# Half of the mode weights, and the loads queued behind them, issued only once the first mix operand exists

## The reference

```python
x = x + L0(_gn(x))     # _gn: every channel of every image to mean 0, variance 1
x = x + L1(_gn(x))

# L0: spectral convolution
x_ft = rfftn(x, axes=(-2, -1))
blk  = einsum('bimn,hiomn->bhomn', x_ft[:, :, :32, :32], weight)   # a 32 x 32 channel matrix per mode (m, n)
xr   = irfftn(blk put into zeros, s=(64, 64))
out  = einsum('bchw,oc->bohw', xr, fc_w) + fc_b

# L1: 3x3 convolution with a kernel of its own for each image
att  = softmax(sigmoid(mean(x) @ ksm_w.T))                  # 16 candidates
cw   = einsum('bk,koihwc->boihwc', att, dft_weight)         # given as a 3x3 spectrum
out  = (conv(x, clip(ifft2(cw).real), padding 1) + bias) * fbm_scale
```

## Time and profile before

| | before |
|---|---|
| time, median of 3 runs | 139.57 us (138.45 to 140.53) |
| span of the profiled execution | 137.8 us |
| time outside the span, against the median | 1.8 us |
| instructions in the span | 4822 |
| PE busy | 122.5 us, 89% of the span; 2060 matmuls and 2060 weight loads |
| VectorE busy | 87.8 us, 64% |
| ScalarE busy | 70.7 us, 51% |
| GpSimd busy | 52.8 us, 38% |
| moved by DMA | 25.17 MB, mean 183 GB/s |

### The profile page before, as it was taken

How to read it: one execution, slowest core, us unless ns; L and a number is a source line. 1 busy time by engine, 2 the same in 40 slices (tenths; PEclk the granted TensorE clock), 3 DMA queues, 4 the chain that set the end, 5 groups by cost and what they waited for, 6 DMA issues and landing times.

```text
span 137.8 us, 4822 instructions
## 1 busy us (share of the span) xinstructions
PE 122.5 (89%) x2060; PEld 91.8 (67%) x2060; DVE 87.8 (64%) x201; ACT 70.7 (51%) x143; POOL 52.8 (38%) x44
## 2 busy tenths in 40 slices
PE   0799997969997969979999979989999999999970
PEld 0799997869996959979999969873323432223230
DVE  0077696879996743553357685999873789922340
ACT  0468458538965336523317775644998329311100
POOL 7993000009999999999600550130500000000000
PEclk9999999999999999999999999999999999999997
DMA  3999999999500036787876899887989968884477
GB/s 90 268 272 257 233 222 357 302 384 399 204 5 7 0 81 156 171 203 165 181 164 153 172 178 153 180 202 164 168 184 175 211 156 189 195 191 105 104 162 143
DMA packets 71892, 25.17 MB, mean 183 GB/s; under 512 B 67904, under 2 KB 68160, under 8 KB 71872
## 3 DMA queue, kind: packets, MB, share of 16 engines
q1 hardware_dynamic: 70784, 24.62, 77.2%
q10 hardware_dynamic: 1088, 0.26, 0.9%
HBM read 14.38 MB, written 4.19 MB: 135 GB/s over the span
## 4 chain that ended last, share of the span: by engine, by line
PE 86%; issue 5%; DVE 3%; DMA 2%; ACT 0%; SPq 0%
PE slot L1050 27%; PE slot L882 14%; PE slot L963 11%; PE slot L978 8%; PE slot L941 6%; PE slot L952 5%; PE slot L908 3%; PE aggp L1008 3%; PE slot L904 3%; DMA x_buf<-x 2%; PE small L904 1%; PE aggp L904 1%; DVE kern L780 1%; PE aggp L941 1%; PE small L892 1%
## 5 line engine op out<-in xcount | busy, mean ns | idle before, releaser
L1050 PE MATMUL slot<-y_buf,conv_w 128*32 128x512 f32 (+1 forms) x136 | 31.7, 603 | 0.0
L1050 PE MATMUL slot<-w_buf,conv_w 128*32 128x512 f32 (+1 forms) x136 | 31.7, 603 | 0.0
L882 PE MATMUL slot<-cst,x_buf 128*64 128x64 f32 x512 | 19.0, 241 | 5.3 <-DMA x_buf<-x 4.5
L882 PEld LDWEIGHTS slot<-cst,x_buf 128*64 128x64 f32 x512 | 18.4, 154 | 5.6 <-issue 5.5
L821 DVE TENSOR_TENSOR bd_buf<-slot,q_buf 128x512 f32<-128x512 f32 (+1 forms) x17 | 11.0, 670 | 9.3 <-PE slot L1050 9.1
L1050 PEld LDWEIGHTS slot<-y_buf,conv_w 128*32 128x32 f32 x136 | 8.3, 109 | 12.6 <-issue 12.0
L441 POOL TENSOR_TENSOR x_buf<-y_buf 128x1024 f32<-128x1024 f32 x4 | 7.7, 1934 | 22.5 <-DVE y_buf L709 22.5
L978 PE MATMUL slot<-cst,t_buf 128*128 128x128 f32 x128 | 15.5, 278 | 0.8 <-issue 0.8
L978 PEld LDWEIGHTS slot<-cst,t_buf 128*128 128x128 f32 x128 | 14.7, 192 | 1.4 <-issue 1.2
L963 PE MATMUL slot<-cst,r_buf 128*64 128x128 f32 x256 | 14.6, 274 | 0.7 <-ACT r_buf L491 0.7
L613 DVE TENSOR_REDUCE row_sq<-q_buf 128x16 f32<-128x1024 f32 (+1 forms) x9 | 9.8, 1097 | 7.7 <-ACT q_buf L459 7.7
(11 more groups left out here) (128 smaller groups left out, 222.7 us busy)
## 6 DMA issues: line engine op xcount, KB each, us to landing
x_buf<-x SPq DMA_DIRECT2D x16, 256.0 KB, 4.3
w_buf<-w_modes SPq DMA_DIRECT2D x16, 256.0 KB, 5.0
x_buf<-x SPq DMA_DIRECT2D x32, 128.0 KB, 3.1
w_buf<-y_buf SPq DMA_DIRECT2D x16, 256.0 KB, 5.9
out<-bd_buf SPq DMA_DIRECT2D x28, 128.0 KB, 2.8
t_buf<-dft_w SPq DMA_DIRECT2D x4, 288.0 KB, 5.3
t_buf<-x_buf SPq DMA_DIRECT2D x8, 128.0 KB, 2.4
r_buf<-x_buf SPq DMA_DIRECT2D x8, 128.0 KB, 3.4
```

The costliest lines, as they stand in the source:

```text
L882: last = pe.matmul(ps[64 * ri:64 * ri + 64, col:col + 64], x_part(k)[:, i, q, :], const("fwd_h")[:, 64 * ri:64 * ri + 64], start=True, sto ...
L1050: last = pe.matmul(ps[32 * j:32 * j + 32, 32 * u0:32 * u1], cw[r][:, b, k, :], src, start=(k == terms[0][0]), stop=(k == terms[-1][0]))
```

## The change

SyncE's program gets one wait. Before the loads of the third ml (mix 2) it waits until VectorE has counted the first operand. The first eight loads of mode weights and the late constants stay where they were; the last eight, the four of `dft_w` and the one of `params` stand behind the new wait, since SyncE issues in order.

```diff
             for ml in range(4):
+                if ml == 2:
+                    sp.wait_ge(bd_ready, 1)
                 for q in range(4):
                     sp.dma_start(modes[:, ml, 8 * q:8 * q + 8].rearrange("p n xo -> p (n xo)"), w_modes[ml, q]
                                  ).then_inc(modes_in[ml], 16)
```

## The result

The changed kernel takes 141.18 us (median of 6 runs, 140.85 to 143.03), the kernel before 139.01 us in the same count (138.01 to 140.61). The ratio is 1.0161, 95% interval 1.0117 to 1.0204, so slower by some 2.2 us, 1.6 to 2.8; whether by more than 2% is left open. The profiled execution has a span of 139.1 us and a time of 140.91, 1.8 us outside the span as forecast.

The account below looks back on a forecast made before the run. PE was taken to bound the kernel, with 86% of the span. The span of 137.8 plus 1.9 for late instruction blocks gave 139.7, and 1.8 us outside it made 141.5 us, range 138.5 to 143.0.

Parts of the forecast that it names:

- The bound, and the holes as missing instructions: PE holds 86% of the span; its "issue" holes of 0.72, 1.22 and 0.85 us are waits for instruction blocks.
- The wait, the landing times, the readers: SyncE resumes at about 31.2 us, last moved byte lands at 42.2, four readers of moved data cost nothing.
- The cover: GpSimd's twelfth step ends at 58.2 us, copies waiting for it start at 61.28: 3 us left.
- The hole before 30.17: PE's early hole of 1.22 us stays, taken as 0; a gain of 1.22 at most kept for the range.
- The later blocks: PE's instruction blocks near 40 and 43 us come late behind moved loads: +1.1 to +3.4 us, taken +1.9.
- case B: Early hole goes, later ones grow: PE resumes at 44.3 to 45.4, +1.1 to +2.2, taken +1.3, 140.9 us; chance 0.20.
- case A: Hole before 30.17 stays, blocks near 40 and 43 late: +1.1 to +3.4, taken +1.9, 141.5 us; chance 0.42.
- The clock: PE's granted clock, 1.00 in each stretch, was not lowered by holes of up to 1.2 us; no cost forecast.
- Theory 2: In the experiments: a late reader, above all GpSimd with its candidate kernels, holds VectorE or copies; +1 us or more.
- the theory: In the experiments: transfers delay PE's instruction blocks; the change removes one delay and makes two.

Follow-up runs that it names:

- GpSimd late: Kernel before with GpSimd's chain on the candidate kernels held until the fifth mix count, transfers unchanged: 139.67, 137.20 and 139.89 us beside 139.28 for before.
- the eight loads left out: Changed kernel without its last eight mode loads, mix 2 and 3 reading the weights of mix 0 and 1: 138.41 us, ratio 0.9929 to before.
- candidate kernels ahead: Changed kernel with the candidate kernel loads and params issued ahead of the new wait, only eight mode loads behind it: 140.12 us, ratio 1.0064 to before.
- before with moved block ends: Kernel before with 16 small products (32 matmuls) added ahead of PE's first work: 139.84 us, ratio 1.0063.
- wait at the last f1: Changed kernel with SyncE waiting for the last f1 instead of the first mix operand: 140.37 us, ratio 1.0066 to before.
- staggered: Changed kernel, but mix 2's loads, candidate kernels and params wait for the last f1, mix 3's for half of mix 1: 139.90 us, ratio 1.0032 to before.
- staggered with moved block ends: The staggered kernel plus 16 small products at PE's start, run twice: 138.80 us, ratio 0.9965, and 140.78 us, ratio 1.0036, to before.
- half of the change: Changed kernel with the wait ahead of only the last four mode loads, mix 2's going out as before: 140.79 us, ratio 0.9959 to before.
- the second measurement: The changed kernel itself, unaltered, measured once more against the kernel before: 141.99 us, ratio 1.0126.
- the changed kernel with moved block ends: Changed kernel plus 16 small products at PE's start: 140.94 us, ratio 1.0081 to before.
- the three with moved block ends among the first eight kernels: 16 small products added at PE's start to the kernel before, the wait at the last f1 and the changed kernel: ratios 1.0063, 1.0083, 1.0081 to before.
- the last: Second run of staggered with moved block ends, against the kernel before: 140.78 us, ratio 1.0036.

## Why the prediction was right, and where it was wrong

*The bound, and the holes as missing instructions.* Right. Moving the program by 32 matmuls moved the holes by 31 or 32, in two kernels.

*The wait, the landing times, the readers.* The wait ended at 31.46 (31.2 forecast), the lull and the busy stretch were there, no engine but GpSimd waited for a moved load. `params`, issued at 37.11 with 6.6 us to landing, was there at 43.7 and read at 46.55; the candidate kernels landed at 43.5, 1.3 us later than the sum had it, and GpSimd's twelfth step ended at 59.3 against 58.2, with the copies at 62.7. The cover held, as the kernel with GpSimd late shows.

*The hole before 30.17.* This is the step that failed: "I take 0, since what was issued first should move first". It went, in both profiles of the changed kernel and with the eight loads left out. In those three, where nothing but the late constants was issued between the request and 30 us, the packet started 2.3 to 3.0 us after it. In four kernels more loads were issued over 1 us ahead of the packet (before, GpSimd late, candidate kernels ahead, before with moved block ends), and it took 3.2 to 4.2 us. That points to traffic issued after the request, but it doesn't prove it. In four others the next loads were issued less than 1 us ahead of the packet or behind it, and can hardly have moved (loads issued at 30.21 moved nothing until 31.0): wait at the last f1 3.5 us, staggered 3.7, staggered with moved block ends 3.2, half of the change 2.2. So 2.2 to 3.7 us without later traffic stand against 3.2 to 4.2 with it, and why the early packet came sooner stays open. What is shown is its price: PE's block lasts 5.4 us (23.55 to 28.95), the packet and the time behind it take 2.4, so a packet that starts within 3.0 us costs nothing.

The Trainium skill (DMA: Bandwidth & Descriptors, Queues, rings and completion order) has each DMA engine take turns between queues, a packet of about 9 to 17 descriptors at a time. If a row of 2 KB is one descriptor, at 82 ns (399 GB/s over 16 engines), a turn is an estimated 0.7 to 1.4 us by that page's figure, not nothing as the prediction had it. On top of the idle 1.1 us that would cover the delays up to about 2.5 us and not those of 2.8 to 4.2. Whether the rest lies in the DMA engines or in memory no run here shows.

*The later blocks.* Right in place, and by the mechanism named. The packets that the prediction had counted back to 36.8 and 40.4 are in the trace of the kernel before, in the windows of 0.1 us from 36.8 and from 40.4:

```profile
q8 instruction: 1, 0.02, 54.9%
q8 instruction: 1, 0.02, 84.4%
```

They start at 36.84 and 40.41, and PE reaches the blocks before at 36.3 and 40.2, so a block is asked for some tenths ahead of PE's own work where PE is not starved. In the changed kernel the packet at 38.2 falls within the 37.7 to 38.7 of case B, PE resumed at 40.65 (40.0 to 41.5) and at 44.81 (44.3 to 45.4). What happened is thus case B, given 0.20 and taken at +1.3 and 140.9 us: +1.2 us in the profile beyond the late start. The forecast was case A's, and that its 141.5 lies as near to the median of 141.18 as B's 140.9 is luck. Its +1.9 stood for the two late blocks alone, whose holes grew by 1.36 + 1.06 = 2.4 us, and it left out the 1.22 us that the early hole gave back. Nor is all of the hole in mix 2 the traffic's: with GpSimd late, with the eight loads left out and with the wait at the last f1, where the engines moved 5 to 7 GB/s by then, it was 1.45, 1.29 and 1.47 us. A block that PE enters starved is asked for only then, and that alone costs a hole in the mix.

*The clock.* "Holes of up to 1.2 us did not lower it" was true of the rows and no ground for longer ones. Of the first runs of the changed kernel three had granted clocks of 0.996 to 1.000 and spans of 139.1 to 139.4 us, and those with 0.976 and 0.964 had 140.6 and 141.2; but one with 0.984 had 139.1. In the profile with 0.982, that of the second measurement, half clock cost 1.1 us of PE's own time. Up to 56 us it fell in six profiles, each time behind a hole of 1.31 to 2.59 us in the mix or the `f2` beside it; holes of 1.30 to 2.01 us in other places or profiles were not followed by it. The Trainium skill (TensorE: Matmul & The Clock Gate, What's actually happening) says that the throttled state is the default and activity lifts it, with 1.2 and 2.4 GHz as the only two levels; the 0.50 to 0.52 of these stretches agree. This may account for the upper ones of the changed kernel's runs; how much of its median it makes is not settled.

*Theory 2.* Small, and its mechanism is in the rows. `bconst` at 1.16 us instead of 0.16 delayed `fc` by 0.2 us in the profile after, and 0.17 with GpSimd late alone. VectorE's step and the step of GpSimd beside it, before and after:

```profile
49.01 0.16 DVE L687 TENSOR_TENSOR bconst<-prm 128x1 f32<-128x1 f32 x1
48.18 1.25 POOL L399 TENSOR_SCALAR bd_buf<-bd_buf 128x384 f32<-128x384 f32 x1
...
50.58 1.16 DVE L689 TENSOR_TENSOR bconst<-prm 128x1 f32<-128x1 f32 x1
50.50 1.22 POOL L398 TENSOR_TENSOR bd_buf<-t_buf,bd_buf 128x384 f32<-128x384 f32 x1
```

The slow step ends with GpSimd's. So it is in all 14 profiles: in five GpSimd ran a TENSOR_TENSOR there (after, the changed kernel again and with moved block ends, GpSimd late, half of the change), and `bconst` took 0.74 to 1.16 us, up to its end; in nine it was at its TENSOR_SCALAR steps, and `bconst` took 0.16. `fc_diag` ended 0.1 to 0.3 us behind GpSimd's TENSOR_TENSOR in all 14. The late candidate kernels cost these tenths by moving GpSimd's TENSOR_TENSOR steps beside `bconst`.

*What stays open.* Single holes scatter by 0.5 us and more with the same transfers, so that holes of one profile predict a ratio only to about 0.5%. No kernel here removes the traffic from both critical places and keeps all loads in time, and of those that the theory had faster than before, only the one without its last eight loads was. What makes a packet late beyond full engines, and how much of the 2.2 us lies outside the 1.3 us of the profile's span, is open too.

## What to carry to other kernels

A long unrolled program on PE needs its instructions through the same DMA engines as its data: where PE runs short matmuls fast, look for "issue" holes at a fixed distance in matmuls, find the instruction queue's packets, and count what else is moving when they are asked for. Putting loads off to a later stage moves the collision, and it is worst in the stage that uses up instructions fastest, here the mix (127 matmuls in 2.2 us, against 3.3 to 4.1 us from the end of one hole to the end of the next, with nearly idle engines). A hole can cost a second time, through the clock, as the 1.1 us of the second measurement show.

## What the runs showed of the hardware

- An instruction packet of 16 KB took 0.9 to 1.8 us, once 2.4. After PE had resumed from a hole, the next one started 1.0 to 1.3 us later in idle engines and 1.4 to 4.2 us later in loaded ones, and PE resumed 1.2 to 1.6 us after a packet's end.
- Full engines do not always delay it: at 384 GB/s, 1.9 us after the loads had begun to move (the changed kernel with moved block ends), and at 390 GB/s near their end (staggered, with moved block ends), packets came in time; between, at 391 GB/s, one started 3.0 us after PE had entered the block before.
- After holes of 1.3 to 2.6 us in or beside the mix the granted clock fell in six profiles (candidate kernels ahead, the three with moved block ends among the first eight kernels, the changed kernel again, and the last) to 0.5 for some 3 us. At half clock 107 matmuls of the mix took 3.10 us, where 108 took 1.90 at full clock, and 16 of `f2` 2.76 instead of 2.00.
- A VectorE TENSOR_TENSOR on a 128x1 tile took 0.16 us beside a TENSOR_SCALAR of GpSimd (9 profiles) and 0.74 to 1.16 us beside a TENSOR_TENSOR of GpSimd (5 profiles), ending with it.
